# Three instead of two expert products a step in the last tiles of a recurrence

## The reference

```python
h = layernorm(x) * (1 + ca) + sa
x = x + ga * attn(h)          # a scan over 512 time steps: a state space (64) and a GRU (128)
h = layernorm(x) * (1 + cb) + sb
x = x + gb * ffn(h)           # every token goes to one of 8 experts, 128 -> 512 -> 128, relu
```

## Time and profile before

| | us |
|---|---|
| median of 3 runs | 830.65 (829.54 to 830.8) |
| the profiled execution's own time | 829.97 |
| its span, first to last instruction | 828.1 |
| mean granted TensorE clock | 0.998 |
| start of step 464 (tile 29) | 681.61 |
| start of step 480, of step 496 | 704.75, 727.95 |
| start of step 511, the last of the scan | 749.83 |

### The profile page before, as it was taken

The page is one execution under the profiler, slowest core; times in us unless marked ns, Lnnn a source line. Parts: engine busy times, 40 slices in busy tenths (PEclk is TensorE's granted clock), DMA queues, the critical chain, the costliest instruction groups (busy, mean ns, idle before and its releaser), DMA issues.

```text
span 828.1 us, 20385 instructions
## 1 busy us (share of the span) xinstructions
PE 806.4 (97%) x6316; PEld 754.5 (91%) x6316; DVE 445.7 (54%) x2708; ACT 387.6 (47%) x2689; POOL 116.4 (14%) x206
## 2 busy tenths in 40 slices
PE   9999999999999999999999999999999999998777
PEld 6999999999999999999999999999999999997666
DVE  5444444455555555555555555555555555556435
ACT  5444444444555445455555444555544455544232
POOL 2001111111010011111111111111111112210202
PEclk9999999999999999999999999999999999999999
DMA  8723000504322000062221001622110342223731
GB/s 318 272 83 125 6 4 5 207 6 177 124 72 74 11 11 11 11 224 90 79 81 46 18 11 45 236 81 75 54 49 11 110 148 88 87 87 110 260 106 45
DMA packets 46748, 75.72 MB, mean 91 GB/s; under 512 B 6284, under 2 KB 28626, under 8 KB 46514
## 3 DMA queue, kind: packets, MB, share of 16 engines
q1 hardware_dynamic: 40338, 68.07, 23.0%
q0 software_dynamic: 1984, 4.07, 1.8%
q10 hardware_dynamic: 4320, 2.30, 1.0%
HBM read 14.31 MB, written 21.04 MB: 43 GB/s over the span
## 4 chain that ended last, share of the span: by engine, by line
PE 95%; issue 1%; ACT 1%; ACTq 1%; DVE 0%; DMA 0%; DVEq 0%
PE s_bank L1101 15%; PE nr_bank L1213 15%; PE nr_bank L1217 15%; PE z_bank L1222 14%; PE y_bank L1148 8%; PE hid_bank_b L1113 6%; PE hid_bank_a L1135 5%; PE hid_bank_b L1135 4%; PE work L1169 2%; PE hid_bank_a L1125 1%; PE s_bank L1088 1%; PE nr_bank L1076 1%; PE work L1172 1%; PE work L1184 1%; PE nr_bank L1080 1%
## 5 line engine op out<-in xcount | busy, mean ns | idle before, releaser
L641 ACT ACTIVATE r_fac<-nr_bank 128x8 f32<-128x8 f32 x512 | 91.1, 178 | 282.0 <-PE nr_bank L1213 280.7
L950 DVE TENSOR_TENSOR_SCAN nr_bank<-r_fac,nr_bank 128x16 f32<-128x16 f32 x512 | 99.9, 195 | 206.6 <-PE nr_bank L1217 204.1
L1101 PE MATMUL s_bank<-s_ring,ws_sb 128*128 128x128 f32 x1024 | 207.1, 284 | 0.0
L1217 PE MATMUL nr_bank<-h_ring,w_sb 128*128 128x32 f32 x1024 | 200.1, 279 | 0.0
L1222 PE MATMUL z_bank<-h_ring,w_sb 128*128 128x32 f32 x1024 | 200.0, 279 | 0.0
L1213 PE MATMUL nr_bank<-h_ring,w_sb 128*128 128x16 f32 x1024 | 188.4, 260 | 0.0
L1213 PEld LDWEIGHTS nr_bank<-h_ring,w_sb 128*128 128x128 f32 x1024 | 152.6, 188 | 27.1 <-DVE h_ring L958 18.3
L958 DVE TENSOR_TENSOR_SCAN h_ring<-z_fac,h_ring 128x24 f32<-128x24 f32 x512 | 106.3, 208 | 127.6 <-ACT h_ring L665 124.1
L1101 PEld LDWEIGHTS s_bank<-s_ring,ws_sb 128*128 128x128 f32 x1024 | 158.5, 191 | 7.0 <-issue 1.8
L1222 PEld LDWEIGHTS z_bank<-h_ring,w_sb 128*128 128x128 f32 x1024 | 155.7, 192 | 0.0
L1217 PEld LDWEIGHTS nr_bank<-h_ring,w_sb 128*128 128x128 f32 x1024 | 155.6, 192 | 0.0
(11 more groups left out here) (170 smaller groups left out, 1098.1 us busy)
## 6 DMA issues: line engine op xcount, KB each, us to landing
wx<-w_all SPq DMA_DIRECT2D x66, 578.0 KB, 3.3
rows<-zeros SPq DMA_DIRECT2D x3, 4096.0 KB, 13.6
xs_sb<-rows SPq DMA_DIRECT2D x66, 64.0 KB, 2.4
w_all<-in_w SPq DMA_DIRECT2D x2, 2048.0 KB, 15.3
rows<-y_sb SPq DMA_DIRECT2D x49, 64.0 KB, 1.6
x_sb<-in_x SPq DMA_DIRECT2D x1, 1920.0 KB, 8.8
out<-o_sb SPq DMA_DIRECT2D x20, 64.0 KB
rows<-y_sb ACTq DMA_DIRECT2D x17, 64.0 KB, 2.3
```

The lines of the kernel that those rows point to most:

```text
L641: nc.scalar.activation(r_fac[:, t % 2, :, 1], r_cols(q, t), ACT.Sigmoid).then_inc(rn_ready, 1)
L950: nc.vector.tensor_tensor_scan(pairs, r_fac[:, k, :, :].rearrange("p b k -> p (b k)"), pairs, 0.0, ALU.mult, ALU.add).then_inc(pre_n_ready, 1)
L1101: return mm(s_cols(g, width=S_WIDE), ws_sb[:, 0:P], s_ring[:, pq, pt, :], start=False, stop=True, skip_group_check=True)
L1217: mm(n_pairs(q, t, N_WIDE)[:, :, 0], w_sb[:, W_HH + 2 * P:W_HH + 3 * P], h[:, 0:N_WIDE], start=False, stop=True, skip_group_check=True).th ...
```

## The change

```diff
     def room(u):
         if u >= NT * T:
             return 3 if u < NT * T + T else 2
-        return ROOM - taken(u)
+        return ROOM + (u >= 29 * T) - taken(u)
```

## The result

The change makes the kernel a little slower: 832.55 us median (831.95 to 833.01, 7 runs) against 830.65 for the kernel before in the same session (829.37 to 831.31, 7 runs), ratio 1.0026, interval 1.0014 to 1.0038, or 1.9 us. A second measurement gave 1.0022 (1.0013 to 1.0031). Forecast was 833.9, 3.2 us over the kernel before.

The account below looks back on a forecast made before the run. TensorE was taken to bound the kernel, nearly level with the scan's recurrence in the loop. Loop +8.0 us and tail -4.8 sum to +3.2: 833.2 for the profiled execution, 833.9 median, range 829.3 to 840.0.

Parts of the forecast that it names:

- the rival "no difference": Whole kernel: loop costs 6 us, tail gains 5 to 6, giving 829.7 to 832 us; chance 0.20.
- The slack of a step: Loop: a two-product step leaves TensorE 0.10 us of slack, so a third product makes it 1.57 us.
- The products of the change: Loop, tiles 29 to 31: 75 more halves on TensorE, less the slack, cost 4.05 us.
- The waits for ScalarE: Loop: X and A wait for late ScalarE relus and copies; with a VectorE pairing, waits together cost 4.0 us.
- the further delay that I had taken over from the earlier trace: Steps 468, 484, 500, 503: 0.42 us from X's late start at 1.60 to the next L1213, giving 2.02 us.
- the third term: Step 7 of tiles 29 and 30: DVE relu beside output-tile instructions delays the scan, 0.25 us twice, 0.5 us.
- The lower bound of nothing: Loop waits: they might cost nothing if ScalarE fits its work in; upper bound 6 us, 4.0 taken.
- the fast rival: Whole kernel: ScalarE serves waits earlier, loop costs only 4.0 us, tail gives 6.1; 828.5 us, chance 0.10.
- The tail: After the loop: slots 54 to 56 start earlier, slot 56 at 18.2 instead of 22.97; gain 4.8 us.
- the charge for the clock: Tail: clock falls at 6 to 10 us; some ten products dearer, 2.1 us, mostly hidden, 0.9 charged.
- The lower bound given for the gain: Tail: gain of only 1.9 us if load collision and low clock both cost full price.
- The rival in which it stays low to the end: Tail: clock stays at half up to the dense stretch at 800, +9 us more, 843 us; chance 0.10.

Follow-up runs that it names:

- the two rules on places: Changed kernel with items moved on a step where ScalarE would be late: first rule splits pairs (830.63 us, 0.9988), second covers every late source (829.46 us, 0.9980).
- the added product alone: Kernel before with one zero-weight product more in each of steps 464 to 507, nothing moved: 835.48 us against 830.98, ratio 1.0049.
- the order with split pairs: Changed kernel, X not sharing a step with the first C before it, A not at t = 5 behind a late X: 830.63 us, ratio 0.9988.
- the two traces of the best: Changed kernel with three items a step only from tile 31 and late-source items moved on, run twice: 824.79 and 824.44 us, ratios 0.9933 and 0.9940 against kernel before.
- the one comparison on a common chip: Changed kernel with twelve hold-clock matmuls in steps 514 to 521 against changed kernel without: 831.82 and 832.74 us, ratios 1.0011 and 1.0022 to kernel before.
- the start at tile 31: Changed kernel with three items a step only from tile 31 instead of tile 29: 828.95 us against 830.98 for the kernel before, ratio 0.9970.

## Why the prediction was right, and where it was off

**The direction and its reason held.** A cost inside the scan of +7.0 us (forecast +8.0) stands against a gain behind it of 5.1 (forecast 4.8). It was close: 832.55 lies 0.55 us above the upper end of the rival "no difference", the loop of 7.0 stands halfway between that rival's 6 and the forecast's 8.0, and the tail of 5.1 within that rival's 5 to 6.

**The slack of a step: right.** Steps with 14 halves take 1.56 us in the changed kernel (1.57 forecast). The products of the change were set at 4.05 us; the two rules on places leave some 3.7 for them, and the added product alone takes 4.5 with 88 halves where the change adds 75. The term was some 0.3 too high.

**The waits for ScalarE: right in place and cause**, 4.0 forecast, some 3.3 measured by taking them away. The four steps with C, C and X take 1.97 us (2.02 forecast): s follows X without the further delay that I had taken over from the earlier trace rows. Steps 469 and 485 take 2.03 (2.04 forecast), step 501 1.82 (1.57 + 0.25). Too dear was the third term, the pairing on VectorE in step 7 of tiles 29 and 30, set at 0.25 us twice. In step 471 it put the scan L950 at 696.92, 0.90 us into step 472, where steps 497 and 498 of the kernel before have 0.57 and 0.67, but TensorE was hardly held up: step 472 takes 1.60 us and step 488 too, against 1.54 and 1.53 in the order with split pairs, which has the same number of halves there. That is 0.06 or 0.07 each. The lower bound of nothing, on which the fast rival rested, is excluded.

**The tail.** Slot 54 was to start its X at 10.2 us and its A at 10.7: 10.0 and 10.9. It was to be its token rows that set it: they did. Slot 55's A was set at 14.0 ahead of the charge for the clock: 14.5. Slot 56 at 18.2: 18.9. What lies behind slot 56 was said to be unchanged at 55.3; it is 54.3 in the changed kernel and 52.2 and 52.8 in the two traces of the best. That assumption failed, by 1 us here, and it was luck that it made up for the 0.7 us by which slot 56 came late: without it the tail would have gained 4.1. The lower bound given for the gain, 1.9, doesn't come out of its terms either: 14.9, 3.3 and 2.1 put slot 56 at 20.3, a gain of 2.7. The cause of the shorter stretch stays open; y stores, output stores, loads and expert products share this stretch, and their order in ScalarE's queue shifts with every step number.

**The clock: it fell where I said** (6 to 10 us after step 511 began; 6.35) and its price, set at 0.9 us, is 0.9 by the medians (0.75 by the means) in the one comparison on a common chip. Twelve products ran at the low clock where some ten were expected: the clock was back 6.6 us after X of slot 54, not 3 to 5.5. The Trainium skill's warning about idle gaps between bursts of matmuls ("TensorE: Matmul & The Clock Gate", "Why this matters for your kernels") agrees with this trace: the granted clock is 0.50 from 764.28 to 774.52, after 3.3 us without a matmul. The rival in which it stays low to the end is out: it returned while slots 54 and 55 kept TensorE busy for 6.4 of 6.5 us.

**What I had not seen** is how unequal the two sides are. I compared the whole change with nothing. Slot 54 did not start before 10.7 us in any trace, since the dispatch and SP's loads take that long; with 23 to 26 items left in that time it starts at 12.0 to 12.3, so they cost 1.2 to 1.5 us there. The 23 items that the change moves and the start at tile 31 doesn't cost 4.6 us in the loop (75.2 against 70.6), emptied the gap and lost the clock. The theory "the gap is set by the dispatch and the loads" was in my prediction; its consequence for the amount was not.

## What to carry to other kernels

Before moving work out of a stretch, find what bounds the stretch once the work is gone, and move only as much as shortens it; what is left there is mostly hidden, and here it kept TensorE's clock up. In a loop that is nearly balanced, the price of one more product has two parts: its own time less the slack, and the waits it makes by bringing an item closer to the one it needs from another engine. The two were about equal here (3.7 and 3.3 us), and the second went away by rules on places: 2.3 us of it with the same items in the loop, the rest with two of 104 items pushed behind it.

## What was not expected of the hardware

With the clock held through the gap it fell all the same later on, at 800.2, though TensorE had had work in the 4 us before: it was busy 1.79 of them, with a wait of 1.22 us and one of 0.82 us that ended at 800.36. In the kernel before a single wait of 1.22 us ahead of slot 54 left it up. So here the clock went in a stretch that was not empty, and one long wait alone had not cost it elsewhere.

What shortens the stretch behind slot 56 to 52.2 us in the best kernel is not settled. In the run with the clock held ScalarE's output store stood in front of a relu there and waited for VectorE; the best kernel's TensorE has one wait of over 0.6 us behind the start of slot 56 (1.13 in one trace, 1.48 in the other), where the changed kernel has four (0.76 to 0.79) and the kernel before four (0.73 to 1.17). The fastest execution of the plain start at tile 31 has two (0.80 and 0.86) and takes 52.64 us. That the order of ScalarE's stores makes the difference is argued from these traces, not shown by a run of its own.
